# Output-projection weight loads issued from GpSimd's DMA queue in place of SyncE's (recurrent layer with an expert FFN, 8 cores)

## The reference, cut to what matters

```python
logits = x @ W_router
expert_idx = jnp.argmax(logits, axis=-1)
h = jnp.einsum('th,ehi->tei', x, W1) + b1            # 4 experts, 1024 -> 4096
h = jax.nn.gelu(h, approximate=False)
onehot = jax.nn.one_hot(expert_idx, E, dtype=x.dtype)
intermediate = jnp.einsum('te,tei->ti', onehot, h)
y = intermediate @ Wo + bo + x                       # 4096 -> 1024
y = _layer_norm(y, ln_gamma, ln_beta)
# outside: g = silu(y);  result = x + s * g
```

## Time and profile before

| | |
|---|---|
| median of 11 runs | 3310.88 us |
| lowest of them | 3305.41 us |
| the profiled execution's own time | 3316.09 us |
| its span on the slowest core (core 6) | 3314.2 us |
| shortest span of the other cores | 3279.2 us |
| PE busy | 2878.2 us (87%) |
| DVE, ACT, POOL busy | 706.1, 470.1, 212.1 us |

### The profile page before, as it was taken

The page is one execution under the profiler, slowest core; times in us unless marked ns, Lnnn a source line. Parts: engine busy times, 40 slices in busy tenths (PEclk is TensorE's granted clock), DMA queues, the critical chain, the costliest instruction groups (busy, mean ns, idle before and its releaser), DMA issues.

```text
span 3314.2 us, 32444 instructions; the slowest of 8 cores (3279.2 to 3314.2 us)
## 1 busy us (share of the span) xinstructions
PE 2878.2 (87%) x13127; PEld 1267.7 (38%) x13376; DVE 706.1 (21%) x1289; ACT 470.1 (14%) x733; POOL 212.1 (6%) x285
## 2 busy tenths in 40 slices
PE   0247877886999999999999999999999999999994
PEld 0113433332444444444444444444444344444442
DVE  0326756661002100310111012002200210031003
ACT  1122222210001110011002011101110111102001
POOL 1025342400000000000000000000000000000000
PEclk9878888898999999999999999999999999999997
DMA  9999999914444544444354435443544444344442
GB/s 132 105 130 126 130 134 156 114 30 166 150 142 157 159 155 152 164 141 156 133 181 143 162 127 180 154 149 133 185 153 149 168 142 163 141 161 144 156 144 81
DMA packets 262385, 476.14 MB, mean 144 GB/s; under 512 B 204700, under 2 KB 204700, under 8 KB 216988
## 3 DMA queue, kind: packets, MB, share of 16 engines
q1 hardware_dynamic: 88640, 408.99, 38.8%
q0 software_dynamic: 173600, 65.07, 18.3%
HBM read 482.44 MB, written 81.79 MB: 170 GB/s over the span
## 4 chain that ended last, share of the span: by engine, by line
PE 72%; DVE 1%; DMA 1%; issue 1%; ACT 1%; DVEq 0%; SPq 0%; ACTq 0%; POOL 0%; POOLq 0%
PE pre L627 27%; PE pmb L627 27%; PE y2a L648 7%; PE y2b L648 7%; DMA w1sl<-w1s 1%; PE pmb L634 1%; PE pre L634 1%; DVE y L684 0%; DVE y L680 0%; DVEq L96 0%; PE y2b L653 0%; DVE maskedA L729 0%; PE pmu L572 0%; PE y2a L653 0%; ACT g_bf L766 0%
## 5 line engine op out<-in xcount | busy, mean ns | idle before, releaser
L627 PE MATMUL pre<-maskedA,w1sl 128*128 128x512 bf16 x4007 | 909.9, 382 | 30.1 <-DVEq L96 12.8
L627 PE MATMUL pmb<-maskedA,w1sl 128*128 128x512 bf16 x4015 | 902.0, 379 | 4.4 <-issue 0.2
L627 PEld LDWEIGHTS pre<-maskedA,w1sl 128*128 128x128 bf16 x4096 | 393.9, 99 | 515.2 <-issue 68.3
L627 PEld LDWEIGHTS pmb<-maskedA,w1sl 128*128 128x128 bf16 x4096 | 390.3, 98 | 482.4 <-issue 29.2
L648 PE MATMUL y2a<-interA,wosl 128*128 128x512 bf16 x1007 | 244.1, 401 | 2.1 <-ACTq L96 1.1
L648 PE MATMUL y2b<-interA,wosl 128*128 128x512 bf16 x1007 | 224.4, 379 | 0.9
L723 DVE COPY mask_bf<-pmb 4x512 bf16<-4x512 bf16 x8 | 3.3, 412 | 959.1 <-PE pmb L592 959.1
L162 POOL DMA_DIRECT2D w1s<-w x256 | 188.4, 778 | 268.9 <-issue 268.9
L790 ACT ACTIVATE interA<-pmb 128x512 bf16<-128x512 f32 x128 | 76.4, 597 | 862.0 <-PE pmb L634 862.0
L790 ACT ACTIVATE interA<-pre 128x512 bf16<-128x512 f32 x128 | 76.4, 597 | 861.2 <-PE pre L634 861.0
L456 PE MATMUL pj<-xn_fm,wfT 128*128 128x512 bf16 x504 | 127.4, 412 | 81.4 <-ACT f_fm L243 51.8
(11 more groups left out here) (119 smaller groups left out, 1392.2 us busy)
## 6 DMA issues: line engine op xcount, KB each, us to landing
w1sl<-w1s SPq DMA_DIRECT2D x256, 1024.0 KB, 5.7
wosl<-wos SPq DMA_DIRECT2D x64, 1024.0 KB, 6.2
w1s<-w POOLq DMA_DIRECT2D x256, 128.0 KB, 18.9
x_a<-x SPq DMA_DIRECT2D x8, 2048.0 KB, 15.4
x_b<-x SPq DMA_DIRECT2D x8, 2048.0 KB, 17.4
out<-y POOLq DMA_DIRECT2D x8, 2048.0 KB, 7.0
wos<-wo POOLq DMA_DIRECT2D x8, 1024.0 KB, 47.4
xnbf_s<-xn_fm SPq DMA_DIRECT2D x8, 1024.0 KB, 22.7
```

Of the source, the lines that this page charges most:

```text
L627: ins = te.matmul(pre4[b][:, :], w1sl[gi % 2][:, off:off + 128], maskedA[:, (e * KC + k) * TT:(e * KC + k + 1) * TT], start=first, stop=False)
```

## The change

The eight `wosl` loads of a tile are taken out of SP's queue and put into POOL's, ahead of the wait for that tile's store. Sizes, buffers and the semaphores waited for and raised are the same.

```diff
@@ stage B, SyncE, in the loop over t, behind the 32 w1sl loads
-                        for h in range(KC):
-                            wi_ = t * KC + h
-                            W(sy, "wo_F", wi_ - 1)
-                            ti(sy.dma_start(out=wosl[wi_ % 2][:, :],
-                                            in_=wos[:, h * I_FF:(h + 1) * I_FF]),
-                               "wo_R%d" % (wi_ % 2), 16)
                         W(sy, "sv_p", t)
                         ti(sy.dma_start(out=s_b[:, :], in_=ss_s[t * 128:(t + 1) * 128, :]),
                            "s_sb", 16)
@@ stage B, GpSimd
                     W(g, "bar", 5)
                     for t in range(NT):
+                        for h in range(KC):
+                            wi_ = t * KC + h
+                            W(g, "wo_F", wi_ - 1)
+                            ti(g.dma_start(out=wosl[wi_ % 2][:, :],
+                                           in_=wos[:, h * I_FF:(h + 1) * I_FF]),
+                               "wo_R%d" % (wi_ % 2), 16)
                         W(g, "sv_out", t + 1)
                         W(g, "st_out", 16 * t)
```

## The result

The changed kernel takes 3366.99 us (median of 12 executions) beside 3315.68 us for the kernel before (47). The ratio is 1.0108, 95% interval 1.0087 to 1.0130: slower by 1.1%. (Both medians include executions in which one die ran at a lower clock; the ratio leaves these out.) On the 3310.9 us from which I forecast that is 3347 us, against 3312 in a range up to 3330. The forecast of no change was wrong: the loss is clear of the noise, and the time lies above the range.

The account below looks back on a forecast made before the run. TensorE's matmuls were taken to bound the kernel, so moved loads count only where TensorE waits. The terms 0 + 1.6 + 0 + 0 gave +1.6 us on the 3310.9 us median: 3312 us, range 3302 to 3330.

Parts of the forecast that it names:

- The 48 slabs on the heels of `wo_F`: Output projection: six `wosl` loads per tile, issued by POOL, land 5.70 us after `wo_F` against 7.12 available; cost 0.
- DVE's hold on POOL: Output projection: delay of POOL's load issues by DVE's casts and masking, put at 0; half a microsecond would still fit.
- Rival A: Output projection waits for its weights because POOL's loads land too late: 3339 us, mild form 3321; chance 0.17.
- The two slabs behind the store: Middle of seven tiles: the next `w1sl` lands after 6.5 to 7.65 us, needed at 7.5; 0 taken, 14 us at worst.
- The silence behind SP's issue: Middle of each tile: time without a byte after SP issues `w1sl`, taken as 1.0 to 2.15 us.
- The shared transfer: Middle of each tile: `w1sl`'s 1.05 MB at an even share of 382 GB/s, taken as 5.5 us.
- rival B: Middle of each tile: slabs behind the store collide with `w1sl`, 14 us plus 1.6, so 3327 us; chance 0.10.
- The start: Start of stage B: tile 0's two early slabs delay TensorE's first group by 1.6 us, bounds 0 to 5.4.
- The tiles' starts: Starts of tiles 1 to 6: waits for the first `w1sl` slab stay near 11.5 us in sum; change taken as 0.
- rival C: Tiles' starts: first slab comes sooner because 3 MB left the queue ahead of it; 3305.5 us, or 3301; chance 0.15.

## Why the prediction was wrong

- **The 48 slabs on the heels of `wo_F`: right.** They land 5.3 us after their issue on the mean of the cores' means, as they did from SP (5.3), and inside the 4.6 to 6.2 that were named (5.70 from `wo_F` less 0.69 of reaction would be 5.0); the longest is 7.2. POOL issues 0.54 us behind the matmul that raises the signal, where 0.69 was taken, and 0.46 behind SP. Waits: 0.3 us. DVE's hold on POOL: none to be seen, as taken. Rival A did not come.
- **The two slabs behind the store: the step that failed.** "in time, or 0.15 us late. ... I take 0, since 382 GB/s is the row where two loads really ran at once." The seven groups lost 27.9 us. Three terms of it were off. The silence behind SP's issue was taken from loads that met an idle queue (1.0 to 2.15 us); beside 2 MB of another queue it is 3.8. The shared transfer took 6.3 us (10.1 less 3.8) where 5.5 stood. And a wait was priced at its own length: the matmuls behind the longer waits, at a granted clock of 0.80 in the group shown, added 8.4 us to 19.5. What the first two have in common: an even share was taken from 1.0 to 2.15 us on, but the slabs had been issued 6.1 us ahead of slab 18, and about one megabyte of them went first. The mechanism was rival B, at 0.10, with a price of 14 us for what is 28; the row that came nearest to a warning was the 10.3 us of the second of two loads issued together, a load behind another, though in one queue.
- **The start: the mechanism right, the size off.** 1.6 us were taken, 3.0 measured, inside the bounds of 0 to 5.4.
- **The closing drain: not in the sum at all.** 5.2 us on the path that sets the end (4.2 net of the shorter tail), 82 ns for each DMA moved to POOL.
- **The tiles' starts: 0 was taken, and holds within 1 us.** The waits there did fall, from 9.3 to 4.2 us, which looked like rival C. But the two sums ahead of them grew by 4.4 us. Here are the rows of the changed kernel at the end of tile 1, and of the kernel before at the end of tile 0:

```profile
1385.77 2.81 PE L661 MATMUL pmu<-p_bf,ones_bf 128*128 128x512 bf16 x8 [2.35 <-DVEq L96]
1388.37 2.70 PE L666 MATMUL psq<-g_bf,ones_bf 128*128 128x512 bf16 x8
1391.67 3.61 PE L627 MATMUL pre<-maskedA,w1sl 128*128 128x512 bf16 x16 [0.60 <-DMA w1sl<-w1s]
```
```profile
1076.61 1.89 PE L661 MATMUL pmu<-p_bf,ones_bf 128*128 128x512 bf16 x8 [2.09 <-DVEq L96]
1078.34 1.89 PE L666 MATMUL psq<-g_bf,ones_bf 128*128 128x512 bf16 x8
```

TensorE arrives later and so waits less; sums and first group together differ by 1.0 us in seven tiles. The mask and projection ahead of them are 4.5 us shorter. Why the slower matmuls moved from the one place to the other stays open.

Why SP's load gets no byte for over 3 us is not settled either. What the packet records do show is who goes first: at slab 18's issue 1.1 to 2.4 MB of the other queue were still to move (means of the five kernels that have the silence), and 1.0 to 1.4 MB of them moved before slab 18's first byte. From there on the queues run side by side, in the changed kernel at about 200 GB/s each. The Trainium skill's page "DMA: Bandwidth & Descriptors", section "Queues, rings and completion order", says that each DMA engine serves the queues that have work in turn, packet by packet, and that a packet is typically 9 to 17 descriptors. No run here shows the engines' turns. A slab of POOL's adds 144 packet records to the trace, nine for each of the 16 engines. Were one turn such a share of a slab, it would last 1.05 MB / 394 GB/s = 2.7 us, and with the 1.1 us of an idle queue the silence would be up to 3.8 us, an estimate near the 3.3 to 4.0 measured; but with turns of that size slab 18's own share would then follow in one piece on each engine, and its transfer took 6.3 us. So the rule is neither borne out nor refuted by these traces.

## What to carry to other kernels

A queue's order is also its priority: an urgent load is safe only because someone wrote the loads that can wait behind it, and moving a part to another queue gives that order up. So look, for each load moved, at what the other queues have in flight when an urgent load is issued, not only at whether the moved load itself is in time. Where a stretch must carry prefetches, issue them behind the urgent load, and look for waits at which a queue stands with free buffers behind it: that was the 0.4% to be had here.

## What the hardware showed that I had not expected

- A load issued beside 1 to 2 MB of another queue's had 3.3 to 4.0 us without a byte on the mean, against 1.1 us alone, whether the other queue was POOL's or ACT's and whether it was loading or storing; about one megabyte of the other queue's went first. Issued 0.52 us ahead of 2 MB of POOL's, a load had 1.2 us.
- POOL's drain at the end of the program takes 0.70 us with 8 DMAs of its own in the stage and 82 ns more for each further one (5.92 us with 72).
- A wait of 2.8 us on the mean ahead of a group cost 1.2 us more in the matmuls behind it (8.4 us in seven), and not evenly: 39 groups of 56 took 9.03 us with part at 1.2 GHz, 17 took 7.38 with none.
